# The end of a fused two-layer kernel: last block's mix moved ahead of its predecessor's second pair, its tiles turned by another path, the last pair's products reordered

## The chip, the core and the metric

The kernel runs on one core of one Trainium2 chip. The metric is device time in microseconds (us); the kernel before takes 696.96 us, the median of three runs (696.9 to 697.5).

## What is computed

Two layers follow one another on 8192 tokens of 512 features. The first adds a random-feature attention to its input and normalises; the second adds a magnitude (real and imaginary part of a product with cosines and sines) and normalises again.

```python
dot_products = jnp.einsum('...d,rd->...r', xw, ab[:, None] * gs)
correction = (0.5 * jnp.sum(xw * xw, axis=-1))[..., None] * (ab * ab)
return 1.0 / math.sqrt(NUM_RFS) * AB * jnp.exp(dot_products - correction)
...
return jnp.einsum('bsr,or->bso', feats, weights)
...
real = jnp.einsum('bti,io->bto', x, jnp.cos(theta + theta_noise))
imag = jnp.einsum('bti,io->bto', x, jnp.sin(phi + phi_noise))
return jnp.sqrt(real * real + imag * imag)
...
x = _layernorm(x + _L0_attn_ref(x, L0_attn_input_weights, L0_attn_xis, L0_attn_proj_matrix), axis=-1)
x = _layernorm(x + _L0_ffn_ref(x, L0_ffn_theta, L0_ffn_phi, L0_ffn_theta_noise, L0_ffn_phi_noise), axis=-1)
```

## The kernel before

The tokens are worked in 16 blocks of 512 (`NB` is 16), a block in four tiles of 128 tokens, the tiles in two pairs. In this document **e** is block 14, `NB - 2`, and **b** is block 15, the last. "(e,1)" is the second pair of e, "(b,0)" the first pair of b. Each engine has its own instruction list, written by hand, and runs it strictly in order; semaphores named after what they count join the lists. So a wait holds back all that stands behind it on its engine.

A block goes through these stages.

- **Mix** (L1001 to L1003, TensorE): features times weights, 12 matmuls for each tile into `token_ps`. VectorE adds the input (`residual1`, L1409) to give `z`, and takes its statistics (L1380, L1384) for the second normalisation.
- **Project** (L945 to L947, TensorE): the next block's features. The last block has none.
- **Turn**: the second layer needs `z` transposed. In all blocks from the third up to e, VectorE turns 32x32 squares of a pair (`turn_squares`, L1615), SyncE stores them to DRAM in four transfers (`store_squares`, L310) and fetches them back in three (`fetch_halves`, L317 to L319). In b, TensorE transposes each tile into `turn_ps` (`turn`, L1012, four transposes a tile) in between its other work.
- **Products** (L1119 to L1121, TensorE): a pair's two real and two imaginary tiles come from seven quarter products M1 to M7 instead of eight, six matmuls each (both operands are split into a high and a low part). Their left operands are quarters of the turned pair and four **half sums** of them (VectorE, L1620 to L1625). ScalarE rounds the high parts (L814 and L829; L819 and L825 in b), VectorE takes the low parts (L1276).
- **Joins** (VectorE): M1 is copied by ScalarE (L836, `copy_first`); then U, V, W and the four results C11, C12, C21, C22 are made by one addition each. `joined` counts them in order, so whoever waits for C21 waits for all that are joined before it. A bank of a product is free for the next pair when its joins have read it.
- **Magnitude and normalisation**: ScalarE squares a tile (L840), GpSimd or VectorE adds the squares (`pair_sum`, L470 on GpSimd), ScalarE takes the root (L718), the residual is added (L474 or L1605), VectorE takes statistics, GpSimd makes scale and shift for a pair in four small instructions (`pair_scale2`, L481 to L487), ScalarE scales into `o_tile` (`norm2`, L724) and SyncE stores.

In the last block the magnitude is worked tile by tile, and pieces of it go to all three engines (L879 to L929 on ScalarE, L527 to L548 on GpSimd, L1703 to L1846 on VectorE). TensorE's order at the end of before is: mix and project of e, pair (e,0), pair (e,1), mix of b with its turning in between, pair (b,0), pair (b,1).

## Time and profile before

| | us |
|---|---|
| median of three runs | 696.96 |
| lowest and highest run | 696.9, 697.5 |
| profiled execution, first to last instruction (span) | 694.6 |
| TensorE busy | 683.2 |
| VectorE busy | 598.5 |
| ScalarE busy | 461.6 |
| GpSimd busy | 202.2 |

The span is that of one profiled execution; it leaves out what lies before the first and behind the last instruction. A profile row gives a start in us from the span's start. A row that stands for several instructions covers them all. "Idle before" in brackets is how long the engine waited, and for whom.

### The profile page before, as it was taken

The page shows a single profiled execution, that of the slowest core. Times are in us where ns is not written, and L with a number is a line of the kernel's source. Part 1 is how long each engine was busy: PE and PEld are TensorE (multiplying, and loading weights), DVE is VectorE, ACT ScalarE, POOL GpSimd, SP SyncE. Part 2 cuts the span into 40 slices and gives each one's busy share as a digit, 9 for nine tenths or more (in the row PEclk, how much of TensorE's full clock was granted, in tenths as well). Part 3 has the DMA queues.
Part 4 walks back from the last instruction along what each step waited for, and adds up shares of the span by engine and source line. Part 5 has one row for each costly group of instructions (what it writes and reads, how often), then busy time and mean ns, then how long its engine had stood idle before and what let it go on. Part 6 is the DMA issues. An engine that isn't in the chain of part 4 may idle for free.

```text
span 694.6 us, 10316 instructions
## 1 busy us (share of the span) xinstructions
PE 683.2 (98%) x3026; PEld 564.2 (81%) x3026; DVE 598.5 (86%) x968; ACT 461.6 (66%) x698; POOL 202.2 (29%) x257
## 2 busy tenths in 40 slices
PE   9999999999999999999999999999999999999994
PEld 7888888878888888888888888888888888888883
DVE  6788999888889888889998887999888898988786
ACT  7868998395666758566674865757485675846446
POOL 5772304105041140503214040320405032050414
PEclk9999999999999999999999999999999999999998
DMA  8861031462826447182654708365380835534011
GB/s 311 234 137 61 15 121 63 116 202 43 211 82 146 157 113 204 31 214 88 142 160 104 213 23 216 94 123 179 95 222 15 213 104 121 181 79 119 0 61 61
DMA packets 168788, 88.10 MB, mean 127 GB/s; under 512 B 112576, under 2 KB 139200, under 8 KB 168768
## 3 DMA queue, kind: packets, MB, share of 16 engines
q1 hardware_dynamic: 167472, 85.51, 45.3%
q0 software_dynamic: 1152, 2.10, 1.8%
q10 hardware_dynamic: 144, 0.26, 0.1%
q8 instruction: 8, 0.13, 0.1%
q14 instruction: 12, 0.10, 0.0%
HBM read 57.41 MB, written 30.44 MB: 126 GB/s over the span
## 4 chain that ended last, share of the span: by engine, by line
PE 92%; DVE 3%; DMA 2%; issue 1%; ACT 1%; SPq 1%; POOL 0%; POOLq 0%; DVEq 0%; ACTq 0%
PE token_ps L1002 8%; PE token_ps L1003 8%; PE token_ps L1001 8%; PE token_ps L1119 6%; PE token_ps L1120 6%; PE token_ps L1121 6%; PE project_ps L945 5%; PE project_ps L947 4%; PE project_ps L946 4%; PE project_ps L1119 4%; PE project_ps L1120 4%; PE project_ps L1121 4%; PE turn_ps L946 3%; PE turn_ps L947 3%; PE turn_ps L945 3%; PE turn_ps L1120 3%
## 5 line engine op out<-in xcount | busy, mean ns | idle before, releaser
L470 POOL TENSOR_TENSOR plain_late<-plain_late 128x1024 f32<-128x1024 f32 x26 | 67.2, 2584 | 264.0 <-ACT plain_late L840 264.0
L1001 PE MATMUL token_ps<-W_hi,F_hi 128*128 128x512 f32 x256 | 99.7, 389 | 0.0
L1003 PE MATMUL token_ps<-W_hi,F_lo 128*128 128x512 f32 x256 | 99.6, 389 | 0.0
L1002 PE MATMUL token_ps<-W_lo,F_hi 128*128 128x512 f32 x256 | 99.6, 389 | 0.0
L724 ACT ACTIVATE o_tile<-plain_late,shift,rstd 128x512 f32<-128x512 f32 x56 | 42.6, 809 | 59.2 <-POOL shift L487 54.8
L718 ACT ACTIVATE plain_late<-plain_late 128x1024 f32<-128x1024 f32 x28 | 29.7, 1062 | 74.7 <-POOL plain_late L470 73.3
L1119 PE MATMUL token_ps<-T_hi,zT_hi 128*128 128x512 f32 x170 | 66.4, 390 | 0.5 <-DVE zT_lo L1276 0.5
L1121 PE MATMUL token_ps<-T_hi,zT_lo 128*128 128x512 f32 x170 | 66.2, 389 | 0.0
L1120 PE MATMUL token_ps<-T_lo,zT_hi 128*128 128x512 f32 x170 | 66.1, 389 | 0.0
L610 ACT ACTIVATE F_hi<-plain_expo,ab 128x512 fp32r<-128x512 f32 x62 | 44.7, 720 | 32.0 <-DVE plain_expo L1281 31.7
L840 ACT ACTIVATE plain_late<-plain_late 128x1024 f32<-128x1024 f32 x54 | 55.1, 1056 | 14.2 <-DVE plain_late L1693 11.1
L1276 DVE TENSOR_TENSOR zT_lo<-plain_zT_lo,zT_hi 128x1024 fp32r<-128x1024 f32 (+1 forms) x54 | 59.0, 1095 | 3.6 <-ACT zT_hi L814 0.5
L945 PE MATMUL project_ps<-xT_hi,gs_hi 128*128 128x512 f32 x144 | 56.8, 394 | 0.1
L1001 PEld LDWEIGHTS token_ps<-W_hi,F_hi 128*128 128x128 f32 x256 | 48.1, 188 | 10.0
L1003 PEld LDWEIGHTS token_ps<-W_hi,F_lo 128*128 128x128 f32 x256 | 48.1, 188 | 10.0
L947 PE MATMUL project_ps<-xT_hi,gs_lo 128*128 128x512 f32 x144 | 56.1, 390 | 0.0
L1002 PEld LDWEIGHTS token_ps<-W_lo,F_hi 128*128 128x128 f32 x256 | 48.1, 188 | 9.9
L946 PE MATMUL project_ps<-xT_lo,gs_hi 128*128 128x512 f32 x144 | 56.1, 389 | 0.0
L1409 DVE TENSOR_TENSOR z<-token_ps,x_tok 128x512 f32<-128x512 f32 x64 | 43.7, 685 | 13.2 <-PE token_ps L1003 11.5
L1436 DVE BATCH_NORM_STATS2 stats<-plain_late 128x6 f32<-128x512 f32 x56 | 37.4, 688 | 13.3 <-POOL plain_late L474 12.8
L1276 DVE TENSOR_TENSOR F_lo<-plain_F_lo,F_hi 128x1024 fp32r<-128x1024 f32 (+1 forms) x38 | 42.1, 1139 | 3.1 <-ACT plain_F_lo L611 3.1
L945 PE MATMUL turn_ps<-xT_hi,gs_hi 128*128 128x512 f32 x112 | 44.0, 393 | 0.0
(284 smaller groups left out, 1790.9 us busy)
## 6 DMA issues: line engine op xcount, KB each, us to landing
x_tok<-in_x SPq DMA_DIRECT2D x16, 1024.0 KB, 6.1
out_tokens<-o_tile SPq DMA_DIRECT2D x62, 256.0 KB, 2.8
plain_xT_lo<-in_xT SPq DMA_DIRECT2D x14, 1024.0 KB, 8.8
turned_pair<-plain_late SPq DMA_DIRECT2D x104, 128.0 KB, 2.8
plain_zT_lo<-turned_pair SPq DMA_DIRECT2D x26, 256.0 KB, 2.8
plain_zT_lo<-turned_pair SPq DMA_DIRECT2D x52, 128.0 KB, 2.8
norm_bc<-token_norms SPq DMA_DIRECT2D x15, 256.0 KB, 3.2
plain_T_hi<-in_gsT SPq DMA_DIRECT2D x4, 256.0 KB, 3.6
```

Source lines behind the costliest of these rows:

```text
L470: pool.tensor_tensor(parts[:, p, :, 0, :], parts[:, p, :, 0, :], parts[:, p, :, 1, :], ALU.add).then_inc(sum_made, 2)
L840: nc.scalar.activation(parts[:, p, i, :, :], parts[:, p, i, :, :], ACT.Square).then_inc(square_done, 2)
L945: nc.tensor.matmul(o, gs_hi[:, c, cols], rhs_hi[:, c, :], start=(c == 0), stop=False)
L946: nc.tensor.matmul(o, gs_hi[:, c, cols], rhs_lo[:, c, :], start=False, stop=False)
L947: return nc.tensor.matmul(o, gs_lo[:, c, cols], rhs_hi[:, c, :], start=False, stop=(c == C - 1))
L1001: nc.tensor.matmul(o, F_hi[:, c, cols], W_hi[:, c, :], start=(c == 0), stop=False)
L1002: nc.tensor.matmul(o, F_hi[:, c, cols], W_lo[:, c, :], start=False, stop=False)
L1003: return nc.tensor.matmul(o, F_lo[:, c, cols], W_hi[:, c, :], start=False, stop=(c == C - 1))
L1119: nc.tensor.matmul(o, left[0][i], right[0][i], start=(i == 0), stop=False)
L1120: nc.tensor.matmul(o, left[0][i], right[1][i], start=False, stop=False)
L1121: last = nc.tensor.matmul(o, left[1][i], right[0][i], start=False, stop=(i == H - 1))
L1276: return tt(dst, whole, hi.bitcast(F32), ALU.subtract)
```

## The change

It leaves all blocks before e as they are, and e too up to the joins of (e,0). From there on:

- TensorE takes the mix of b ahead of (e,1). The order is then mix and project of e, (e,0), mix of b, (e,1), (b,0), (b,1).
- b is turned as the other blocks are, by VectorE and DRAM; the 16 transposes of TensorE are gone. The turned squares go to the place of `xT`, the sum of b's first residual is written over its input (`last_z` is `x_tok[:, 1]`), and the turned second pair lands where the projection matrix was (`gs_hi`, `gs_lo`).
- The products of (b,1) come in the order M1, M6, M7, M4, M5, M2, M3, before M1, M2, M4, M6, M7, M5, M3; those of (b,0) in the order of all other blocks. Banks are those of all other blocks.
- `pair_sum(e, 1)` goes from GpSimd to VectorE. On ScalarE the root of tile 3 goes ahead of the last square.
- All lists from there to the end are written anew in `last_steps`.

```diff
-        QUARTER_ORDER_LAST = ["M1", "M2", "M4", "M6", "M7", "M5", "M3"]
+        QUARTER_ORDER_LAST = ["M1", "M6", "M7", "M4", "M5", "M2", "M3"]
-        JOIN_ORDER_LAST = ["U", "C11", "V", "C21", "C22", "W", "C12"]
+        JOIN_ORDER_LAST = ["U", "V", "C21", "C22", "W", "C11", "C12"]
...
+            store_squares(last, 0, last_squares)
+            fetch_halves(last, 0, last_raw)
+            store_squares(last, 1, last_squares)
+            store_out(last - 1, 0)
+            store_out(last - 1, 1)
+            fetch_halves(last, 1, last_raw)
+            store_out(last - 1, 2)
+            store_out(last - 1, 3)
...
-            pair_sum(b - 1, 1)
...
-            pool.wait_ge(square_done, 2 * C * NB + SQUARE_CREDIT - 1)
+            pool.wait_ge(square_done, 2 * C * NB + SQUARE_CREDIT - 2)
...
+                square_tile(e, 0, 1)
+                square_tile(e, 0, 0)
+                pair_roots(e, 0)
+                copy_first(e, 1)
+                norm2(e, 0)
+                norm2(e, 1)
+                round_halves(b, 0, last_hi, last_raw)
+                round_half_sums(b, 0, last_hi, last_raw)
+                square_tile(e, 1, 1)
+                copy_first(b, 0)
+                square_tile(e, 1, 0)
+                round_halves(b, 1, last_hi, last_raw)
+                round_half_sums(b, 1, last_hi, last_raw)
+                pair_roots(e, 1)
+                norm2(e, 2)
+                norm2(e, 3)
+                square_tile(b, 0, 1)
+                square_tile(b, 0, 0)
+                act.wait_ge(out_made, C * e + 3)
+                copy_first(b, 1)
...
-                square_part("C11", 0, 0)
+                square_part("C21", 1, 1)
...
-                square_part("C21", 1, 1)
                 square_part("C22", 1, 0)
+                square_part("C11", 0, 0)
+                root_tile(1, 1, last_sum_made, 1)
                 square_part("C12", 0, 1)
-                root_tile(1, 1, last_sum_made, 1)
                 root_tile(1, 0, sum_made, C * b + 3)
...
+                for name in QUARTER_ORDER_LAST:
+                    if name == "M1":
+                        pe.wait_ge(halves_lo_made, 2 * s + 2)
+                        pe.wait_ge(joined, joins_done(e, 1, JOIN_ORDER, "U"))
+                    else:
+                        if name == "M6":
+                            pe.wait_ge(half_sums_lo_made, 2 * s + 2)
+                        pe.wait_ge(joined, joins_done(b, 0, JOIN_ORDER, *BANK_READ[name]))
+                    one_product(1, name, last_hi, last_lo)
...
+                residual1(b, 1, 1, last_z)
+                turn_squares(b, 0, last_z, last_squares)
...
+                join_c12()
+                landed_half_sums(b, 1, last_raw)
+                split_halves(b, 1, last_hi, last_lo, last_raw)
+                pair_sum(e, 1)
+                join_u, join_v, join_w, join_c11, join_c12, join_c21, join_c22 = joins_of(b, 0)
+                join_u()
+                split_half_sums(b, 1, last_hi, last_lo, last_raw)
+                join_v()
+                pair_residual2(e, 1)
+                pair_stats2(e, 1, 0)
+                join_c22()
+                join_w()
+                pair_stats2(e, 1, 1)
+                pair_stats2_made(e, 1)
+                pair_moments2(1)
+                join_c11()
+                join_c21()
+                join_c12()
+                sum_tile(0, 1, 2)
+                sum_tile(0, 0, 4)
```

VectorE's list where b's first pair is joined, before. The first row is a low part of (b,1), L1620 to L1625 are its half sums, the others the joins of (b,0), in the order U, C11, V, C21, C22, W and C12:

```order
L1276 TENSOR_TENSOR zT_lo<-turn_ps1,zT_hi 128x256
L1667 TENSOR_TENSOR plain_late<-token_ps1,plain_late 128x512
L1682 TENSOR_TENSOR plain_late<-project_ps0,plain_late 128x512
L1620 TENSOR_TENSOR plain_zT_lo<-turn_ps1,plain_zT_lo 128x256
L1621 TENSOR_TENSOR plain_zT_lo<-turn_ps0,plain_zT_lo 128x256
L1623 TENSOR_TENSOR plain_zT_lo<-plain_zT_lo,turn_ps0 128x256
L1625 TENSOR_TENSOR plain_zT_lo<-turn_ps0,plain_zT_lo 128x256
L1674 TENSOR_TENSOR plain_late<-token_ps2,plain_late 128x512
L1693 TENSOR_TENSOR plain_late<-token_ps0,plain_late 128x512
L1698 TENSOR_TENSOR plain_late<-token_ps3,plain_late 128x512
L1678 TENSOR_TENSOR plain_late<-token_ps3,plain_late 128x512
L1687 TENSOR_TENSOR plain_late<-project_ps1,plain_late 128x512
```

There the joins of (b,0) share the list with work for (b,1) alone. The same place of the changed kernel (its own line numbers: L1620 is now every join, L1571 `pair_sum(e, 1)`, L1575 the residual of (e,1), L1406 and L1354 its statistics):

```order
L1246 TENSOR_TENSOR gs_lo<-plain_gs_lo,gs_hi 128x768
L1571 TENSOR_TENSOR plain_late<-plain_late 128x1024
L1620 TENSOR_TENSOR plain_late<-token_ps1,plain_late 128x512
L1246 TENSOR_TENSOR gs_lo<-plain_gs_lo,gs_hi 128x1024
L1620 TENSOR_TENSOR plain_late<-token_ps2,plain_late 128x512
L1575 TENSOR_TENSOR plain_late<-z,plain_late 128x1024
L1406 BN_STATS stats2<-plain_late 128x6
L1620 TENSOR_TENSOR plain_late<-token_ps3,plain_late 128x512 x2
L1406 BN_STATS stats2<-plain_late 128x6
L1354 BN_AGGR mv2<-stats2 128x2 x2
L1620 TENSOR_TENSOR plain_late<-project_ps0,plain_late 128x512
L1620 TENSOR_TENSOR plain_late<-project_ps1,plain_late 128x512
```

What moved: the sum of squares, the residual and the statistics of (e,1) now stand between the joins of (b,0), the last row of which is C21.

ScalarE's list from (b,1)'s half sums to the last scaling of a tile, before (L829 rounds, L840 squares a tile of (b,0), L836 copies M1, L879 are roots, L904 and L908 mean and variance of tile 1, L899 squares of one part, L918 scalings):

```order
L829 ACTIVATE zT_hi<-plain_zT_lo 128x1024
L840 ACTIVATE plain_late<-plain_late 128x2x512
L836 ACTIVATE plain_late<-project_ps0 128x512
L840 ACTIVATE plain_late<-plain_late 128x2x512
L879 ACTIVATE plain_late<-plain_late 128x512 x2
L904 ACTIVATE unused,mv2<-plain_late 128x512
L899 ACTIVATE plain_late<-plain_late 128x512
L908 ACTIVATE unused,mv2<-plain_late,mv2 128x512
L899 ACTIVATE plain_late<-plain_late 128x512 x3
L879 ACTIVATE plain_late<-plain_late 128x512 x2
L918 ACTIVATE o_tile<-plain_late,shift2,rstd2 128x512 x2
```

The same place of the changed kernel (L824 rounds, L729 is the root of (e,1), L735 scales tiles 2 and 3 of e, L833 squares (b,0), L829 copies M1, L898 roots, L911 and L915 mean and variance, L906 squares):

```order
L824 ACTIVATE gs_hi<-plain_gs_lo 128x1024
L729 ACTIVATE plain_late<-plain_late 128x1024
L735 ACTIVATE o_tile<-plain_late,shift2,rstd2 128x512 x2
L833 ACTIVATE plain_late<-plain_late 128x2x512 x2
L829 ACTIVATE plain_late<-turn_ps1 128x512
L898 ACTIVATE plain_late<-plain_late 128x512 x2
L911 ACTIVATE unused,mv2<-plain_late 128x512
L906 ACTIVATE plain_late<-plain_late 128x512
L915 ACTIVATE unused,mv2<-plain_late,mv2 128x512
L906 ACTIVATE plain_late<-plain_late 128x512 x2
L898 ACTIVATE plain_late<-plain_late 128x512
L906 ACTIVATE plain_late<-plain_late 128x512
```

What moved: e's last root and two scalings now stand ahead of the squares of (b,0) and of the copy of M1 of (b,1), and one root stands ahead of the last square.

## Rows read from the trace of the kernel before

**Rows 1.** The page: busy us, share of the span and instructions of each engine.

```profile
PE 683.2 (98%) x3026; PEld 564.2 (81%) x3026; DVE 598.5 (86%) x968; ACT 461.6 (66%) x698; POOL 202.2 (29%) x257
```

**Rows 2.** Timeline, TensorE, 633 to 685 us: start, duration, engine, line, operation.

```profile
633.26 0.39 PE L1119 MATMUL token_ps<-cos_hi,zT_hi 128*128 128x512 f32 x1
...
660.24 0.39 PE L1003 MATMUL token_ps<-W_hi,F_lo 128*128 128x512 f32 x1
...
668.57 1.03 PE L1012 MATMUL turn_ps<-ident,z 128*128 128x128 f32 x8
...
684.50 0.39 PE L1121 MATMUL project_ps<-low_sin_hi,zT_lo 128*128 128x512 f32 x1
```

**Rows 3.** Timeline, VectorE, block e: turning, residual, half sums, low parts.

```profile
617.94 1.25 DVE L1615 STREAM_TRANSPOSE plain_late<-z 128x1024 f32<-128x1024 f32 x1
619.11 1.18 DVE L1605 TENSOR_TENSOR plain_late<-z,plain_late 128x1024 f32<-128x1024 f32 x1
...
628.69 0.42 DVE L1620 TENSOR_TENSOR plain_zT_lo<-plain_zT_lo 128x256 f32<-128x256 f32 x1
...
630.34 0.96 DVE L1276 TENSOR_TENSOR zT_lo<-plain_zT_lo,zT_hi 128x768 fp32r<-128x768 f32 x1
...
631.88 1.22 DVE L1276 TENSOR_TENSOR zT_lo<-plain_zT_lo,zT_hi 128x1024 fp32r<-128x1024 f32 x1
...
634.84 0.43 DVE L1620 TENSOR_TENSOR plain_zT_lo<-plain_zT_lo 128x256 f32<-128x256 f32 x1 [0.56 <-DMA plain_zT_lo<-turned_pair]
```

**Rows 4.** Timeline, SyncE's queue, block e: stores and fetches of the turned pairs.

```profile
619.21 2.25 SPq L310 DMA_DIRECT2D turned_pair<-plain_late  x4
...
623.69 0.38 SPq L317 DMA_DIRECT2D plain_zT_lo<-turned_pair  x1
...
625.39 2.84 SPq L310 DMA_DIRECT2D turned_pair<-plain_late  x4
630.85 0.38 SPq L317 DMA_DIRECT2D plain_zT_lo<-turned_pair  x1
```

**Rows 5.** Timeline, ScalarE: rounding, two squared tiles, two scaled tiles.

```profile
628.31 0.83 ACT L814 ACTIVATE zT_hi<-plain_zT_lo 128x768 fp32r<-128x768 f32 x1
...
645.13 2.01 ACT L840 ACTIVATE plain_late<-plain_late 128x1024 f32<-128x1024 f32 x2 [0.19 <-DVE plain_late L1693]
...
658.25 1.52 ACT L724 ACTIVATE o_tile<-plain_late,shift,rstd 128x512 f32<-128x512 f32 x2 [0.21 <-POOL shift L487]
```

**Rows 6.** Timeline, GpSimd: first and last of a pair's four scale instructions; a tile's sum.

```profile
656.84 0.21 POOL L481 TENSOR_TENSOR var_eps<-mv,damp 128x2 f32<-128x2 f32 x1
...
658.02 0.20 POOL L487 TENSOR_TENSOR shift<-neg_mean,rstd 128x2 f32<-128x2 f32 x1
...
685.28 1.27 POOL L548 TENSOR_TENSOR plain_late<-plain_late 128x512 f32<-128x512 f32 x1 [0.52 <-ACT plain_late L899]
```

**Rows 7.** Timeline, VectorE, the end: joins of the last pair, and what follows.

```profile
680.91 0.69 DVE L1667 TENSOR_TENSOR plain_late<-token_ps,plain_late 128x512 f32<-128x512 f32 x1 [1.16 <-PE token_ps L1121]
681.52 0.68 DVE L1682 TENSOR_TENSOR plain_late<-token_ps,plain_late 128x512 f32<-128x512 f32 x1
682.26 0.69 DVE L1674 TENSOR_TENSOR plain_late<-token_ps,plain_late 128x512 f32<-128x512 f32 x1
...
685.24 0.69 DVE L1687 TENSOR_TENSOR plain_late<-project_ps,plain_late 128x512 f32<-128x512 f32 x1
685.85 0.68 DVE L1711 BATCH_NORM_STATS2 stats<-plain_late 128x6 f32<-128x512 f32 x1
686.63 0.69 DVE L1703 TENSOR_TENSOR plain_late<-plain_late 128x512 f32<-128x512 f32 x1
...
690.90 0.55 DVE L1388 TENSOR_SCALAR z<-plain_late,mv,rstd 128x512 f32<-128x512 f32 x1
```

**Rows 8.** Stretches of 1 us, TensorE: length, busy, granted clock, DMA share, GB/s.

```profile
687.00:688.00 1.00, 0.00 (x0) 0.92 0.00 0
688.00:689.00 1.00, 0.00 (x0) 0.50 0.00 0
```

634 lines of the change are left out of this document (271 added, 363 removed).

## The prediction

> **What bounds the kernel now.** Read the page's busy shares first: TensorE is busy 98% of the span [rows 1], and up to its last product it hardly ever waits. So only two things can shorten the kernel: less work or fewer gaps on TensorE, or a shorter tail behind its last product. Then the timeline of TensorE at the end [rows 2]: the pair (e,0) starts at 633.26, the transposes of b stand between its mix and its products, and the last matmul starts at 684.50 and ends at 684.89. Then VectorE's [rows 7]: the last join C12 starts at 685.24 and the last scaling ends at 691.45. The tail behind TensorE is thus 6.56 us of VectorE, ScalarE and GpSimd, and then the store. Then the other engines' rows for block e [rows 3 to 6], since they give the price of everything that the change puts into b. The span is 694.6 and the median 696.96, so 2.36 us lie around the span; I add the same after.
>
> **TensorE: 2.5 us less, if nothing else holds it.** Matmuls of 512 columns follow each other every 0.227 us (120 from 633.26 to 660.24). From 633.26 to 684.50 there are 216 of them and 16 transposes [rows 2]. Without transposes the rest of the list is 28 products of six matmuls (1.36 each) and four mixes of twelve (2.72 each), 48.97 us in all. From 633.26 that ends at 682.2, with the last matmul's own length at 682.4. Against 684.89 this is 2.5 us less: the slots of the transposes (the last eight take a row of 1.03 us, part of it under the next product [rows 2]) and the slower restart of matmuls behind each group. The mix of b now starts at 642.8, and its features are ready by then, since VectorE's list is unchanged up to the joins of (e,0). Moving it and the new banks cost nothing by themselves.
>
> **The turned pairs through DRAM: just in time.** The second tile of b is mixed at 648.4, its residual ends at 649.2, the turning of the pair takes 1.25 [rows 3] and ends at 650.5. In block e the store's first issue to the fetch's first issue took 4.5 (619.21 to 623.69) and, with more traffic beside it, 5.5 (625.39 to 630.85) [rows 4]; the fetch had landed 4.0 after its first issue (630.85 to 634.84, where VectorE waited for it) [rows 3, 4]. With 4.5 and 3.9 the pair (b,0) lands at 659.1; by the slower rows up to 661. TensorE wants its low parts at 663.2 and those of the half sums at 664.5. The half sums take 1.68, the low parts 0.88, and between them and the second low parts stand two joins: the first is ready at 661.8, the second at 664.1. This fits by 0.4 us, and a slow DMA costs TensorE 0.4 to 0.9, for which slack is to be had further on.
>
> A page of the Trainium skill speaks against this edit: "Vector Engine: DVE Perf Modes" names TensorE as the way for 128x128 transposes whose result may lie in PSUM ("Rules for kernel authors"). The rows agree that TensorE's way is short in latency, and by that rule alone the turning should have stayed there; no row shows what TensorE's own gap is worth once VectorE is full, which is what the following sum is about.
>
> **VectorE's queue: the bound that the change creates.** Before, the end of e and the work on b were spread over 50 us in which TensorE ran as well. Now b's turning, half sums and low parts, and all that (e,1) still needs of VectorE, `pair_sum(e, 1)` too, stand between joins. I went through the five lists from 641 on, row by row: an instruction starts when the one ahead on its engine lets it (a join every 0.61, the next one 0.77 behind its own operand [rows 7]) and 0.08 after what it waits for. The same walk over the kernel before ends the last scaling at 691.47, where the profile has 691.45. For the changed kernel it gives:
>
> - From the landing at 659.1 VectorE works without a stop: half sums 1.68, low part 0.88, joins C22 and W 1.22, low part 1.14, C11, a statistics pass (0.61 like a join [rows 7]) and C21 1.83, four small moments 0.48, C12 0.69. That is 667.05. The half sums of (b,1), landed long before, end at 668.6.
> - ScalarE squares (e,1) as its joins come and can round (b,1) only behind that (some 1.0 for a squared tile, 0.83 for the rounding [rows 5]): 669.3. VectorE loses 0.8 us there.
> - Then low part 0.88, `pair_sum(e, 1)` 1.10, U 0.61, low part 1.14, V 0.61, the residual of (e,1) 1.26 [rows 3], statistics, C22, W 1.83, statistics 0.77, moments 0.16, C11 0.61, C21 0.69: 9.66 us, so **C21 of (b,0) is joined at 679.1**.
> - TensorE has M1, M6 and M7 of (b,1) done at 676.8, and M4 needs the bank that C21 frees. It waits 2.3 us. Its last product ends at 684.85, where it ended before: **the 2.5 us are gone again.**
>
> **ScalarE and GpSimd: the tail gets longer.** The moments of (e,1) come at 677.84. GpSimd's four small instructions take 1.4 (656.84 to 658.22) [rows 6], so ScalarE scales tiles 2 and 3 of e from 679.3 to 680.8 (1.52 [rows 5]) and only then squares (b,0), until 682.7 (2.0 [rows 5]). VectorE, done with its joins at 679.7, waits for these squares, and the copy of M1 of (b,1) is behind them too: U of (b,1) starts at 683.4. Before it started at 680.91, and there it waited for its product; now M6 has been done since 675.6. The seven joins take 4.8, as before 5.0 (680.91 to 685.93), so C12 ends at 688.25 in place of 685.93: **2.3 us later.**
>
> Behind it the roots of (b,0) have also come later; the first ends at 683.8. GpSimd makes their residuals until 686.4, ScalarE the variance of tile 1 until 687.2, GpSimd its scale until 688.4, and only then the sum of squares of tile 3 (1.27 [rows 6]) until 689.65. ScalarE's list now has the root of tile 3 ahead of the last square, so that square starts at 690.3 and the sum of squares of tile 2 on VectorE at 690.99; before it was 686.63 [rows 7]. **Another 2.0 us later.** From there to the end of the last scaling it was 4.82 us (686.63 to 691.45 [rows 7]); the walk itself has 5.16, in both kernels. So the end comes at 695.8 to 696.15 in place of 691.45, 4.4 to 4.7 us later. I take 4.4, since it uses the measured tail.
>
> **The sum.** 694.6 + 4.4 + 2.36 = 701.4.
>
> **What is unknown.** The DMA path: a landing 0.5 earlier (the most that VectorE could use, since it waits 0.5 for it) takes 0.5 off, the slower store of [rows 4] adds 0.8, and with a fetch of 4.6 in place of 3.9, an estimate from the spread of the two stores, 1.5. The walk itself: 0.3 us off in its middle against the profile of before, so perhaps 1 us over this longer queue. TensorE's clock: before, it stayed at its upper level for some 2.9 us after the last matmul (0.92 in the stretch from 687, then 0.50, which is 1.2 GHz [rows 8]). A wait of 2.3 us is a little shorter, with one of over 2.9 the four products left would take 10.9 instead of 5.4 and C12 would end at 691; the tail hides all but 0.8 us of that, since the last square is late anyway. Instruction lists are longer by one unrolled block on TensorE; I count nothing for it.
>
> **The rivals.**
>
> - **As meant: the queues keep up.** Were C21 of (b,0) joined by 676.8, TensorE would end at 682.4, and with the tail of before, 6.56, the end would be at 689.0, 2.5 us sooner: 694.5. The point from which it decides is 2.3 us of VectorE's queue. For it: VectorE was idle at several places before (1.16 us ahead of 680.91 alone [rows 7]). Against it: the walk leaves only 1.3 us of idle time from 658.6 on, and none from 669.4 to 679.7. Chance 0.05.
> - **The wait on M4 comes, the tail stays as it was.** TensorE ends at 684.85, and ScalarE and GpSimd deliver as before: 697.0. It needs ScalarE to have squared (b,0) by 680, while its list puts e's scalings ahead. Chance 0.05.
> - **Forecast**, 4.4 us later, 0.72: 701.4, and by its own bounds 700.3 to 702.6.
> - **Slow turning**, the same with stores and fetches as in the slower rows: 5.9 us later, 702.9. Chance 0.11.
> - **The clock falls** during the wait for C21: 0.8 more, 702.2. Chance 0.07.
>
> **How the numbers follow.** The range, 699.7 to 703.4, holds the forecast and the last two rivals with 0.6 us to spare below and 0.5 above for the walk; the first two rivals lie outside. What counts as a change is 0.2%, or 1.4 us, about what a measurement of this kernel can tell from none. Faster 0.05, same 0.05, slower 0.90.
>
> **What would show it.** In the profile after: TensorE waits for VectorE's C21 at the first matmul of M4 of the last pair, 1.8 to 2.6 us; its last matmul starts at 684 to 685.5. VectorE has no idle time from 669.4 to 679.5, then waits some 2 us for the squares of (b,0). U of (b,1) starts near 683.4, the sum of squares of tile 2 near 691. ScalarE's two scalings of e end near 680.8. I am wrong if U of (b,1) starts before 681.5 or if the end of the last scaling is less than 6 us behind C12; and wrong in the first part if TensorE shows no wait behind M7 of the last pair.

## The result: 0.66% slower, and the profile after

The changed kernel takes 701.89 us (median of six runs, 700.98 to 703.06) against 697.68 for the kernel before measured beside it (six runs): the medians lie 4.2 us apart, and the ratio of the two, with a 95% interval, is 1.0066 (1.0053 to 1.0079). The profiled execution has a span of 699.0 (before 694.6).

The page's busy line answers [rows 1]: TensorE works 2 us less, VectorE 1.3 more, and the kernel is longer. Share of busy time does not explain this; the order of waits does.

```profile
PE 681.1 (97%) x3010; PEld 562.5 (80%) x3010; DVE 599.8 (86%) x969; ACT 459.8 (66%) x694; POOL 199.4 (29%) x256
```

Timeline of TensorE: its two waits from the mix of b on, and its last matmul ([rows 2] has that at 684.50).

```profile
643.21 0.47 PE L1007 MATMUL token_ps<-W_hi,F_hi 128*128 128x512 f32 x1 [0.34 <-DVE plain_late L1620]
...
679.36 0.50 PE L1119 MATMUL project_ps<-T_hi,gs_hi 128*128 128x512 f32 x1 [1.89 <-DVE plain_late L1620]
...
684.73 0.39 PE L1121 MATMUL turn_ps<-low_sin_hi,gs_lo 128*128 128x512 f32 x1
```

The wait of 1.89 is M4 of the last pair, for the join C21 of (b,0).

Timeline of VectorE: second residual of b, statistics of (e,0), the first half sum of (b,0), the first low part of (b,1), the last joins of (b,0), and the tail, which answers [rows 7].

```profile
648.95 0.69 DVE L1379 TENSOR_TENSOR x_tok<-token_ps,x_tok 128x512 f32<-128x512 f32 x1 [0.67 <-PE token_ps L1009]
...
654.73 1.29 DVE L1406 BATCH_NORM_STATS2 stats<-plain_late 128x6 f32<-128x512 f32 x2 [2.37 <-POOL plain_late L486]
...
659.71 0.41 DVE L1588 TENSOR_TENSOR plain_zT_lo<-plain_zT_lo 128x256 f32<-128x256 f32 x1
...
669.78 0.96 DVE L1246 TENSOR_TENSOR gs_lo<-plain_gs_lo,gs_hi 128x768 fp32r<-128x768 f32 x1 [1.02 <-ACT gs_hi L820]
...
678.05 1.25 DVE L1620 TENSOR_TENSOR plain_late<-project_ps,plain_late 128x512 f32<-128x512 f32 x2
...
682.16 0.69 DVE L1739 TENSOR_TENSOR plain_late<-plain_late 128x512 f32<-128x512 f32 x1 [2.26 <-ACT plain_late L833]
...
683.72 1.47 DVE L1620 TENSOR_TENSOR plain_late<-token_ps,plain_late 128x512 f32<-128x512 f32 x2
...
687.75 0.68 DVE L1620 TENSOR_TENSOR plain_late<-turn_ps,plain_late 128x512 f32<-128x512 f32 x1
...
691.04 0.69 DVE L1739 TENSOR_TENSOR plain_late<-plain_late 128x512 f32<-128x512 f32 x1 [2.01 <-ACT plain_late L906]
...
695.30 0.55 DVE L1358 TENSOR_SCALAR z<-plain_late,mv,rstd 128x512 f32<-128x512 f32 x1
```

Read them as one chain. VectorE has no gap between 669.78 and the end of C12 of (b,0) at 679.90; C11 and C21 are the two joins at 678.05. Behind them it waits 2.26 for ScalarE's squares, and ScalarE's own row says why they are late: it scales two tiles of e first, and had waited 6.63 us for GpSimd's shift.

```profile
679.66 1.52 ACT L735 ACTIVATE o_tile<-plain_late,shift,rstd 128x512 f32<-128x512 f32 x2 [6.63 <-POOL shift L499]
681.09 1.99 ACT L833 ACTIVATE plain_late<-plain_late 128x1024 f32<-128x1024 f32 x2
682.98 0.57 ACT L829 ACTIVATE plain_late<-turn_ps 128x512 f32<-128x512 f32 x1
```

So U of the last pair starts at 683.72 (before 680.91), its C12 at 687.75 (before 685.24), the last sum of squares at 691.04 (before 686.63) and VectorE's last scaling ends at 695.85 (before 691.45): 4.4 us. ScalarE's part of that scaling ends 0.12 us behind VectorE's in both kernels.

### The profile page after: what moved, and what is told of

The parts are those of the page before. It is cut to its first block and busy times, and to the rows that moved or that the text cites. A ratio compares the mean times of both kernels' runs of the same rounds, so it can differ in the third digit from the quotient of the medians.

```text
span 699.0 us, 10271 instructions
## 1 busy us (share of the span) xinstructions
PE 681.1 (97%) x3010; PEld 562.5 (80%) x3010; DVE 599.8 (86%) x969; ACT 459.8 (66%) x694; POOL 199.4 (29%) x256
## 5 line engine op out<-in xcount | busy, mean ns | idle before, releaser
L482 POOL TENSOR_TENSOR plain_late<-plain_late 128x1024 f32<-128x1024 f32 x25 | 65.8, 2633 | 261.9 <-ACT plain_late L833 261.9
L735 ACT ACTIVATE o_tile<-plain_late,shift,rstd 128x512 f32<-128x512 f32 x56 | 42.6, 809 | 70.4 <-POOL shift L499 60.3
L729 ACT ACTIVATE plain_late<-plain_late 128x1024 f32<-128x1024 f32 x28 | 29.7, 1062 | 74.4 <-POOL plain_late L482 71.7
L1620 DVE TENSOR_TENSOR plain_late<-token_ps,plain_late 128x512 f32<-128x512 f32 x112 | 74.0, 682 | 3.9
L833 ACT ACTIVATE plain_late<-plain_late 128x1024 f32<-128x1024 f32 x54 | 55.0, 1055 | 21.5 <-DVE plain_late L1620 21.2
L1119 PE MATMUL token_ps<-T_hi,zT_hi 128*128 128x512 f32 x162 | 63.1, 390 | 0.5 <-DVE zT_lo L1246 0.5
L1120 PE MATMUL token_ps<-T_lo,zT_hi 128*128 128x512 f32 x162 | 63.0, 389 | 0.0
L1121 PE MATMUL token_ps<-T_hi,zT_lo 128*128 128x512 f32 x162 | 63.0, 389 | 0.0
L1246 DVE TENSOR_TENSOR zT_lo<-plain_zT_lo,zT_hi 128x768 fp32r<-128x768 f32 (+1 forms) x54 | 58.8, 1089 | 3.4 <-ACT zT_hi L824 0.5
L1379 DVE TENSOR_TENSOR z<-token_ps,x_tok 128x512 f32<-128x512 f32 x60 | 40.9, 685 | 12.4 <-PE token_ps L1009 10.9
L1406 DVE BATCH_NORM_STATS2 stats<-plain_late 128x6 f32<-128x512 f32 x56 | 37.5, 688 | 14.9 <-POOL plain_late L486 14.4
```

What stands on the lines that cost most here:

```text
L482: pool.tensor_tensor(parts[:, p, :, 0, :], parts[:, p, :, 0, :], parts[:, p, :, 1, :], ALU.add).then_inc(sum_made, 2)
L1119: nc.tensor.matmul(o, left[0][i], right[0][i], start=(i == 0), stop=False)
L1120: nc.tensor.matmul(o, left[0][i], right[1][i], start=False, stop=False)
L1121: last = nc.tensor.matmul(o, left[1][i], right[0][i], start=False, stop=(i == H - 1))
L1246: return tt(dst, whole, hi.bitcast(F32), ALU.subtract)
L1620: tt(to, bank_of[name][:, :], to_it, ALU.add).then_inc(joined, 1)
```

## Experiments

Single profiled executions reach the second residual of b up to 3.7 us apart (648.95 in the changed kernel, 652.66 in pool_sum); the wait ahead of b's mix alone differs by up to 1.2 us between kernels whose lists are the same up to there. So I measure each by its **distance**: from the start of the second residual of b (648.95 above, where VectorE waits for TensorE's mix) to the end of the last scaling (695.30 + 0.55). In the changed kernel it is 46.90 us. The ratio beside it is the time against the kernel before. Here are the runs, with the change of the distance against the changed kernel that each theory's text stands for (mix_behind, a single run, is told at the end):

| run | ratio (interval) | distance | against changed | theory had |
|---|---|---|---|---|
| changed kernel | 1.0066 (1.0053 to 1.0079) | 46.90 | | |
| probe_queue | 1.0077 (1.0054 to 1.0099) | 48.10 | +1.20 | +1.2 |
| probe_idle | 1.0074 (1.0051 to 1.0098) | 46.96 | +0.06 | 0 |
| round_first | 1.0056 (1.0039 to 1.0073) | 46.15 | -0.75 | -0.75 |
| root_last | 1.0053 (1.0036 to 1.0071) | 45.62 | -1.28 | -1.4 |
| joins_first | 1.0092 (1.0071 to 1.0113) | 48.21 | +1.31 | +1.4 |
| three_orders | 1.0079 (1.0059 to 1.0098) | 46.04 | -0.86 | -2.1 |
| lists_anew | 1.0064 (1.0049 to 1.0078) | 46.33 | -0.57 | -5.6 |
| pool_sum | 1.0070 (1.0047 to 1.0094) | 47.42 | +0.52 | +0.5 |
| lists_apart | 0.9991 (0.9982 to 1.0000) | 41.35 | -5.55 | -5.5 |
| lists_apart_r | 0.9989 (0.9980 to 0.9998) | 41.60 | -5.30 | -5.9 |
| products_old | 1.0109 (1.0094 to 1.0125) | 48.53 | +1.63 | +0.3 |

The intervals are some 1 us wide on either side, so for the small edits it is the distance that decides, not the ratio: the times alone do not tell probe_queue from probe_idle, and for probe_idle and three_orders the ratio stands above the changed kernel's, with intervals that overlap. The distance comes from one profiled execution each. How well it repeats can be seen where lists are the same: from the second residual of b to M4 of the last pair the changed kernel takes 30.41 us, root_last 30.45 and probe_idle 30.45.

### Is VectorE's queue the bound, and where?

Two statistics passes whose result nobody uses, at two places. In probe_queue:

```diff
                 split_halves(b, 1, last_hi, last_lo, last_raw)
                 pair_sum(e, 1)
+                for k in range(2):
+                    nc.vector.bn_stats(probe_sink[:, k, :], last_z[:, 1, :])
```

> The changed kernel with 1.2 us of work more on VectorE whose result nobody uses: two statistics passes of 512 columns, between the sum of squares of (e,1) and the joins of (b,0), thus in the stretch in which the prediction found VectorE to be the bound. Theory: each microsecond there is a microsecond at the end. TensorE waits 3.1 us ahead of M4 in place of 1.9, the last scaling ends 1.2 us later, ratio 1.0083. Rival: the end is set by the chain of squares, sums and scales on ScalarE and GpSimd, and VectorE has slack; then as the changed kernel, 1.0066.

In probe_idle:

```diff
                 residual1(b, 1, 2, last_z)
+                for k in range(2):
+                    nc.vector.bn_stats(probe_sink[:, k, :], last_z[:, 1, :])
                 pair_stats2(e, 0, 0)
```

> The same 1.2 us of useless statistics passes on VectorE, but ahead of the statistics of (e,0) near 652.4, where it waited 2.4 us for GpSimd's residual. Theory: free, as the changed kernel, 1.0066 (no more than 0.2 us later), since VectorE is the bound only from the low parts of b on. Rival: VectorE is the bound in all of the last two blocks, and these cost as much as the others: 1.0083.

In distance, all of the 1.2 us comes out at the end in the first, none in the second. Timeline of TensorE in probe_queue, M4 of the last pair; the same row was a wait of 1.89:

```profile
683.00 0.50 PE L1120 MATMUL project_ps<-T_hi,gs_hi 128*128 128x512 f32 x1 [2.69 <-DVE plain_late L1621]
```

The wait is 2.69 and not the 3.1 expected, since M6 was held up too and M7 ends 0.4 us later; M4 itself starts 1.20 later, 31.61 behind the second residual of b in place of 30.41.

In probe_idle VectorE's own wait for GpSimd at the statistics of (e,0) shrank from 2.37 to 1.20 us and TensorE's for M4 stayed at 1.92. Of the two places, only the one behind the low part of (b,1) costs time.

probe_idle holds a second experiment that nobody planned. Right behind M4's wait the granted clock fell (0.74 in the stretch from 681, 0.50 in the next), and matmuls came 0.43 apart. Timeline of TensorE in probe_idle, and two stretches (length, busy, granted clock, DMA share, GB/s):

```profile
680.77 0.50 PE L1120 MATMUL project_ps<-T_hi,gs_hi 128*128 128x512 f32 x1 [1.92 <-DVE plain_late L1621]
...
682.04 0.63 PE L1121 MATMUL project_ps<-T_lo,gs_hi 128*128 128x512 f32 x1
...
687.74 0.39 PE L1122 MATMUL turn_ps<-low_sin_hi,gs_lo 128*128 128x512 f32 x1
```

```profile
681.00:682.00 1.00, 1.00 (x4) 0.74 0.00 0
682.00:683.00 1.00, 1.00 (x4) 0.50 0.22 84
```

From M4 to the last matmul it took 6.97 us and not 5.37, so TensorE ended 1.6 us later, and yet the end of the kernel moved by 0.06. So TensorE's end is not what sets the kernel's; what does is shown by the runs on the tail.

### ScalarE's part in that queue

```diff
                 square_tile(e, 1, 1)
                 copy_first(b, 0)
-                square_tile(e, 1, 0)
                 round_halves(b, 1, last_hi, last_raw)
+                square_tile(e, 1, 0)
```

> The changed kernel with ScalarE's rounding of the halves of (b,1) ahead of its square of the first tile of (e,1), as the halves have landed long before. VectorE idled 1.02 us for that rounding at 669.78. By the walk that idle time goes, the whole of VectorE's queue up to C21 of (b,0) moves by 0.75 us, TensorE's wait ahead of M4 shrinks from 1.9 to 1.1 us, and the end comes 0.75 us sooner: ratio 1.0055. Rival: the sum of squares of (e,1) needs that square and becomes what VectorE waits for instead; then nothing is gained, 1.0066.

Timelines of TensorE and VectorE in round_first:

```profile
680.06 0.50 PE L1119 MATMUL project_ps<-T_hi,gs_hi 128*128 128x512 f32 x1 [1.12 <-DVE plain_late L1620]
```

```profile
670.34 0.96 DVE L1246 TENSOR_TENSOR gs_lo<-plain_gs_lo,gs_hi 128x768 fp32r<-128x768 f32 x1
671.34 1.23 DVE L1571 TENSOR_TENSOR plain_late<-plain_late 128x1024 f32<-128x1024 f32 x1
```

The 1.02 of idle time ahead of the low part are gone. The sum starts 1.00 behind the low part in place of 0.87, so the rival holds for 0.13 us. M4 waits 1.12, and the end moves with it.

### The tail behind the last join

root_last puts the last square ahead of the root of tile 3, as before the change:

```diff
                 square_part("C11", 0, 0)
-                root_tile(1, 1, last_sum_made, 1)
                 square_part("C12", 0, 1)
+                root_tile(1, 1, last_sum_made, 1)
```

> The changed kernel with one part undone: on ScalarE the last square (C12 of the last pair) stands ahead of the root of tile 3 again. Theory (each engine's list is walked in order, and the tail is set by what stands ahead of what): the sum of squares of tile 2 on VectorE starts 2.0 us sooner in the walk and the end comes 1.4 us sooner, at about 694.5 instead of 695.85, so some 700.4 in time. Rival (the end is late only because TensorE waits 2 us for the bank of M4): that wait stays, so no change, 701.8.

The sum of squares of tile 2 starts 1.9 us sooner by distance and the end comes 1.28 sooner, although that sum now runs beside one of GpSimd and takes 1.25 in place of 0.69 (the next section has the reason). joins_first moves the joins of (b,0) ahead of what is left of (e,1):

```diff
                 join_v()
-                pair_residual2(e, 1)
-                pair_stats2(e, 1, 0)
                 join_c22()
                 join_w()
+                join_c11()
+                join_c21()
+                pair_residual2(e, 1)
+                pair_stats2(e, 1, 0)
                 pair_stats2(e, 1, 1)
                 pair_stats2_made(e, 1)
                 pair_moments2(1)
-                join_c11()
-                join_c21()
```

> The changed kernel with VectorE's joins C22, W, C11 and C21 of the first pair of the last block moved ahead of the residual and the statistics of block 14's second pair. It takes away TensorE's wait for M4 and leaves all else. Rival (that wait is the loss): TensorE ends 2.3 us sooner and so does the kernel, 699.5. Theory (ScalarE's list holds the squares of the last block behind block 14's two scalings, and these wait for the statistics moved back): TensorE's wait vanishes, its last product ends near 682.5, and yet the first join of the last pair starts 1.4 us LATER, near 685.1, and the kernel takes 1.4 us more, 703.3.

TensorE has no wait for M4 here, its last matmul starts at 683.20 (by distance 2.2 us sooner than in the changed kernel), and the end comes 1.3 us later than in the changed one. VectorE then waits 3.45 for the squares:

```profile
684.17 0.69 DVE L1739 TENSOR_TENSOR plain_late<-plain_late 128x512 f32<-128x512 f32 x1 [3.45 <-ACT plain_late L833]
```

This tells the two halves of the loss apart. The edit is no pure removal of the wait, since it pays for it with later statistics of (e,1). But TensorE ends 2.2 sooner and the kernel 1.3 later, because the squares, and the copy of M1 behind them, hang on those statistics by way of GpSimd and ScalarE. probe_idle is the counterpart: TensorE 1.6 later, the kernel the same.

### Two misses, and what they had in common

three_orders puts both edits together, and the squares of (b,0) ahead of the scaling of e:

```diff
                 pair_roots(e, 1)
-                norm2(e, 2)
-                norm2(e, 3)
                 square_tile(b, 0, 1)
                 square_tile(b, 0, 0)
+                norm2(e, 2)
+                norm2(e, 3)
```

> joins_first, and besides on ScalarE the squares of the last block's first pair ahead of block 14's last two scalings, and the last square ahead of the root of tile 3. Theory: together 2.1 us sooner than the changed kernel, of which 1.4 come from the last square and 0.7 from the two others together, though moving the joins alone costs 1.4 and moving the squares alone would bring only 0.1; the end of the last scaling near 693.8, the time near 699.8. Rival (the pieces simply add up): 1.4 sooner from the square, 1.4 later from the joins, 0.1 sooner from the squares, so the same as the changed kernel, 701.8.

It gained 0.86 and not 2.1. Timeline of GpSimd in three_orders, the last two of the four small instructions of a pair's scale, for (e,1):

```profile
680.43 1.25 POOL L496 TENSOR_TENSOR rstd<-var_eps,neg_half 128x2 f32<-128x2 f32 x1
681.81 0.65 POOL L499 TENSOR_TENSOR shift<-neg_mean,rstd 128x2 f32<-128x2 f32 x1
```

For (e,0) they took 0.70 and 0.20 in the same execution. (Durations on GpSimd are rough in such a profile, but the distance between the two starts grew by the same 0.55.) What ran beside them on VectorE were the sums of squares at 680.44 (0.68) and 681.71 (0.69). ScalarE waited 0.81 for the shift, and the scaling of e and the copy of M1 behind it came that much later. The last sum of squares, beside a sum of GpSimd, took 1.35 in place of 0.69; but root_last has 1.25 there and came out within 0.12 of its walk, so this explains little. Of the 1.2 us that are missing some 0.8 are thus accounted for, and the rest is open.

lists_anew takes new lists for the last two blocks on VectorE and ScalarE, and gives the sum of squares and the residual of (e,1) to GpSimd (L482 and L486 below):

```diff
             b = NB - 1
             pair_scale2(b - 1, 0)
+            pair_sum(b - 1, 1)
+            pair_residual2(b - 1, 1)
```

> The changed kernel with TensorE's list as it is, but the lists of VectorE, ScalarE and GpSimd from the mix of the last block on in another order: GpSimd makes sum of squares and residual of block 14's second pair, the turning of the second pair of the last block comes before statistics that can wait, the joins of the last block's first pair come before what the last pair does not need, and block 14's last two scalings come behind the squares. Theory: with the queues out of the way the 2.5 us that TensorE saves come through in part: the last product ends near 682.8, the last scaling near 690.3 against 691.45 in the kernel before, so 1.2 us sooner than before, 0.2%, ratio 0.998. Rival (the turning through DRAM costs what the transposes did, whatever the order): not sooner than the kernel before, ratio 1.000 or more.

Again a miss, by 5.0 us of distance. Timelines of GpSimd and of VectorE in lists_anew:

```profile
668.65 2.41 POOL L482 TENSOR_TENSOR plain_late<-plain_late 128x1024 f32<-128x1024 f32 x1 [7.03 <-ACT plain_late L835]
674.67 2.40 POOL L486 TENSOR_TENSOR plain_late<-z,plain_late 128x1024 f32<-128x1024 f32 x1 [3.60 <-ACT plain_late L731]
```

```profile
668.82 2.53 DVE L1590 TENSOR_TENSOR plain_gs_lo<-plain_gs_lo 128x256 f32<-128x256 f32 x1 [0.33 <-DMA plain_gs_lo<-turned_pair]
...
674.45 0.68 DVE L1622 TENSOR_TENSOR plain_late<-token_ps,plain_late 128x512 f32<-128x512 f32 x1
675.05 3.10 DVE L1248 TENSOR_TENSOR gs_lo<-plain_gs_lo,gs_hi 128x1024 fp32r<-128x1024 f32 x1
```

A half sum that takes 0.42 elsewhere takes 2.53 and ends 0.3 behind GpSimd's sum (671.06); a low part of 1.22 takes 3.10 and ends 1.1 behind GpSimd's residual (677.07). Both have two operands in SBUF. A join, which has one of them in PSUM, ran beside the start of that residual (674.45 to 675.13) at its usual 0.68. So in such a pair whoever started first went on, and the other stood. My walk knew nothing of it. With that rule in it (an instruction with two SBUF operands on VectorE and one of GpSimd exclude each other), the walk ends lists_anew at 695.3 instead of 689.8; measured, and counted from the changed kernel's second residual of b, it is 695.28. That is a fit after the fact, not yet a test.

The Trainium skill states this in "SBUF — State Buffer" ("SBUF: two separate sides"): VectorE and GpSimd share a pair of ports as an exclusive lock, taken by a VectorE instruction with two SBUF inputs when GpSimd's also reads SBUF, and the later one blocks until the first is done. The trace agrees, 2.53 for 0.42 and 3.10 for 1.22.

### The lock put to the test

pool_sum undoes one part of the change, the move of `pair_sum(e, 1)` off GpSimd. Without the lock that is a relief for VectorE; with it, a loss.

```diff
             b = NB - 1
             pair_scale2(b - 1, 0)
+            pair_sum(b - 1, 1)
...
                 split_halves(b, 1, last_hi, last_lo, last_raw)
-                pair_sum(e, 1)
```

> The changed kernel with one part undone: the sum of squares of (e,1) is GpSimd's again, as before the change; all else stays. GpSimd starts it at about 668.7 and holds it for 2.4 us, while VectorE comes to the low part of (b,1) at 669.4. Theory (VectorE's instructions with two operands in SBUF wait for a long one of GpSimd): that low part takes 2.5 us in place of 0.95, so VectorE gets back the 1.1 us of the sum only to lose 1.6, and the end comes 0.5 us later than in the changed kernel: ratio to the kernel before 1.007. Rival: the two engines do not hold each other up; then VectorE's full queue is 1.1 us shorter and so is the time, ratio 1.005.

Timelines of GpSimd and VectorE in pool_sum:

```profile
672.86 2.40 POOL L482 TENSOR_TENSOR plain_late<-plain_late 128x1024 f32<-128x1024 f32 x1 [10.77 <-ACT plain_late L834]
```

```profile
673.48 2.59 DVE L1247 TENSOR_TENSOR gs_lo<-plain_gs_lo,gs_hi 128x768 fp32r<-128x768 f32 x1 [1.03 <-ACT gs_hi L821]
```

The low part of 0.96 took 2.59, and the end came 0.52 later instead of 1.1 sooner. This is the one edit that tests the lock by itself. (Here too the granted clock fell behind M4's wait, of 2.39 us, and TensorE took 1.6 longer to its end, which again did not show.)

lists_apart is another set of lists, ordered by the walk with the lock in it, with nothing long on GpSimd beside b's halves. Its core on VectorE:

```diff
-                split_halves(b, 0, last_hi, last_lo, last_raw)
                 join_c22()
                 join_w()
-                split_half_sums(b, 0, last_hi, last_lo, last_raw)
                 join_c11()
-                stats1(b, 3, last_z)
                 join_c21()
...
+                split_halves(b, 0, last_hi, last_lo, last_raw)
                 join_c12()
-                landed_half_sums(b, 1, last_raw)
-                split_halves(b, 1, last_hi, last_lo, last_raw)
+                split_half_sums(b, 0, last_hi, last_lo, last_raw)
                 pair_sum(e, 1)
+                landed_half_sums(b, 1, last_raw)
+                pair_residual2(e, 1)
...
                 join_u()
-                split_half_sums(b, 1, last_hi, last_lo, last_raw)
-                join_v()
-                pair_residual2(e, 1)
                 pair_stats2(e, 1, 0)
-                join_c22()
-                join_w()
                 pair_stats2(e, 1, 1)
+                split_half_sums(b, 1, last_hi, last_lo, last_raw)
```

What it does is let (e,1) go first wherever TensorE does not yet wait, so that its statistics, and with them the scaling, are over 5 us sooner (673.41 against 678.14, less the 0.47 by which its second residual of b is later). ScalarE scales e and copies M1 of (b,1) ahead of the squares of (b,0), and takes the last root as root_last does.

> The three lists in a new order again, but now no long instruction of GpSimd (sum of squares, residual) runs while VectorE works on the halves of b: both, for the pair (e,1), are on VectorE. Where the sum of squares runs beside them as in the kernel called lists_anew (VectorE's 0.42 us half sum took 2.53 us beside GpSimd's sum at 668.65, its 1.22 us low part 3.10 us beside GpSimd's residual at 674.67), an instruction of VectorE with two operands in SBUF waited until GpSimd's was over. Theory: that waiting was what lists_anew lost. With it in the walk through the five lists, lists_anew ends its last scaling at 695.3 and not at 689.8, the changed kernel at 696.3, and this one at 690.5 to 691.0, where the kernel before has 691.45: 0.5 to 0.9 us sooner, a ratio to the kernel before of 0.999 (0.998 to 1.000), and some 5.5 us sooner than the changed kernel. Rival: what lists_anew lost lies in the lists or in the way through DRAM; then this one is late like it, at a ratio of 1.005 or more.

Timelines of VectorE and of TensorE in lists_apart:

```profile
666.51 1.23 DVE L1570 TENSOR_TENSOR plain_late<-plain_late 128x1024 f32<-128x1024 f32 x1
667.65 0.42 DVE L1587 TENSOR_TENSOR plain_gs_lo<-plain_gs_lo 128x256 f32<-128x256 f32 x1
...
684.52 0.69 DVE L1619 TENSOR_TENSOR plain_late<-turn_ps,plain_late 128x512 f32<-128x512 f32 x1 [0.74 <-PE turn_ps L1120]
...
690.22 0.55 DVE L1357 TENSOR_SCALAR z<-plain_late,mv,rstd 128x512 f32<-128x512 f32 x1
```

```profile
664.71 0.50 PE L1118 MATMUL token_ps<-cos_hi,zT_hi 128*128 128x512 f32 x1 [0.36 <-DVE zT_lo L1245]
...
684.02 0.39 PE L1120 MATMUL turn_ps<-low_sin_hi,gs_lo 128*128 128x512 f32 x1
```

The last join waits for TensorE again, and TensorE has no wait for M4. The last scaling ends at 690.77, within the 690.5 to 691.0 expected, though this execution reached b 0.47 later than the changed kernel's; the distance, which leaves that out, is 5.55 shorter than the changed kernel's, expected some 5.5. With 696.40 us it is 0.8% faster than the changed kernel and 0.1% faster than the one before, the latter at the edge of what its interval tells from nothing and less than the 0.2% that the prediction counts as a change. It differs from the changed kernel in many places, so it shows that the loss can be had back with b turned through DRAM; how much of the 5.5 us belongs to which move is not shown.

lists_apart_r also gives the residual of (e,1) to GpSimd, with the lists around it adjusted:

```diff
             pair_scale2(b - 1, 0)
+            pair_residual2(b - 1, 1)
...
-                pair_residual2(e, 1)
```

> As lists_apart, but the residual of (e,1) runs on GpSimd, at a moment when VectorE goes from low parts to joins (which read PSUM). By the walk it starts at 670.7, waits 0.7 us for VectorE's low part, and holds VectorE nowhere; the last scaling ends at 690.2 to 690.6, 0.4 us sooner than in lists_apart, ratio 0.998. Rival: VectorE arrives some tenths of a microsecond later than the walk has it, GpSimd's residual is first, and VectorE's next low part waits up to 2.4 us; then it is 1 to 2 us slower than lists_apart, ratio 1.001 to 1.003.

Neither came out in full. GpSimd's residual was the one that waited (2.98 us in place of 2.40, from 671.91), VectorE was held nowhere by it, but the gain of 0.4 did not come: distance 41.60 against 41.35, 696.23 us against 696.40. The two can't be told apart.

### Other parts of the change, undone

products_old restores the order that the last pair's products and joins had before:

```diff
-        QUARTER_ORDER_LAST = ["M1", "M6", "M7", "M4", "M5", "M2", "M3"]
+        QUARTER_ORDER_LAST = ["M1", "M2", "M4", "M6", "M7", "M5", "M3"]
-        JOIN_ORDER_LAST = ["U", "V", "C21", "C22", "W", "C11", "C12"]
+        JOIN_ORDER_LAST = ["U", "C11", "V", "C21", "C22", "W", "C12"]
```

> The changed kernel with one part undone: the products of the last pair in the order of before (M1, M2, M4, M6, M7, M5, M3), and its joins with them. M2 then needs the bank that C11 of (b,0) frees, right behind M1. By the walk TensorE waits for that from 674.2 to 678.5, 4.3 us, in place of 1.9 us ahead of M4, and its last product ends at 687.0 in place of 684.9. If the granted clock stays at its upper level over such a wait, the end comes only 0.3 us later than in the changed kernel, since the last pair's joins wait for ScalarE's copy anyway: 702.2, ratio 1.007. Rival: the clock falls in the wait, as it did some 3 us behind the last matmul of both kernels (0.92 in the stretch from 687 in the kernel before, then 0.50). Then the six products left take 16.3 us in place of 8.2, at worst, and the time is up to 707, ratio 1.010 to 1.015.

The wait is as expected, and the time of 703.97 (1.0109) lies at the low end of the rival's range, but its mechanism came only in part: the clock stayed up all through the wait and fell afterwards, for some of the products. Timeline of TensorE in products_old, and its stretches (length, busy, granted clock, DMA share, GB/s):

```profile
679.59 0.50 PE L1119 MATMUL project_ps<-cos_hi,gs_hi 128*128 128x512 f32 x1 [4.05 <-DVE plain_late L1620]
...
681.58 0.63 PE L1119 MATMUL project_ps<-T_hi,gs_hi 128*128 128x512 f32 x1
682.01 0.63 PE L1120 MATMUL project_ps<-T_lo,gs_hi 128*128 128x512 f32 x1
```

```profile
676.00:680.00 4.00, 0.41 (x2) 1.00 0.01 2
680.00:682.00 2.00, 2.00 (x7) 0.62 0.00 0
682.00:684.00 2.00, 2.00 (x6) 0.53 0.73 262
684.00:686.00 2.00, 2.00 (x10) 1.00 0.03 8
```

From 680.39 to 684.03 nine matmuls took 3.64 us instead of 2.04: 1.6 us lost, which with the 0.3 of the order itself would be 1.9, and 1.63 was measured. Here the loss shows, as TensorE is by then late enough that VectorE's U waits for it (1.05). The new order of products was worth its place: it makes a wait of 4.05 into one of 1.89.

mix_behind leaves the mix of b behind (e,1), with the turning through DRAM kept, and the lists of VectorE and ScalarE put into the order that this asks for; the diff shows TensorE's part:

```diff
                 first_pair(e)
-                pe.wait_ge(F_made, C * (b + 1))
-                for j in range(C):
-                    pe.wait_ge(joined, joins_done(e, 0, JOIN_ORDER, *BEFORE_MIX[j]))
-                    mix(b, j)
...
+                pe.wait_ge(F_made, C * (b + 1))
+                for j in range(C):
+                    pe.wait_ge(joined, joins_done(e, 1, JOIN_ORDER, *BEFORE_MIX[j]))
+                    mix(b, j)
```

> The changed kernel without its first part: b is turned by VectorE and DRAM, but its mix stands behind (e,1), as before. By the walk the pair (b,0) lands only at 671, TensorE waits some 11 us between mix and M1 of (b,0) (663.2 to 674.3), and the last scaling ends 4.5 us later than in the changed kernel, 706.3, if the clock comes back at once; with the clock at its lower level for the first products behind the wait 2 to 6 us more, up to 712. Rival: the changed kernel has lost so much in its queues that the place of the mix is worth little; then at most 1 us more than the changed kernel, 703 or less.

One run: 709.67 us, within the 708 to 712 that the theory gives with the lower clock, and far from the rival's 703. The span is 707.7, 8.7 longer than the changed kernel's. Timeline of TensorE in mix_behind, M1 of (b,0), and its stretches:

```profile
676.06 0.80 PE L1119 MATMUL token_ps<-cos_hi,zT_hi 128*128 128x512 f32 x1 [11.87 <-DVE zT_lo L1246]
```

```profile
664.00:668.00 4.00, 0.19 (x1) 1.00 0.48 128
668.00:676.00 8.00, 0.00 (x0) 0.50 0.97 234
676.00:680.00 4.00, 3.94 (x9) 0.50 0.20 75
```

So the way through DRAM needs the early mix: without it the kernel takes 8 us more than the changed one. The reverse, the early mix with TensorE's own transposes, was not run.

## Why the prediction was right, step by step

- **TensorE 2.5 us less, if nothing else holds it.** Right in kind, a little too much in size. From the last matmul of (e,0) to the last of all it was 41.94 us before (642.56 to 684.50); in joins_first, where no wait for M4 is left, it is 40.06 (643.14 to 683.20), 1.9 less. The wait at the mix takes most of the rest.
- **The mix of b costs nothing by itself.** Not quite: TensorE waits 0.34 there and restarts slower by 0.1, since VectorE comes to U of (e,0) at 642.38 and not at 640.94. "VectorE's list is unchanged" was true, but not enough: its data came later (the last section has what stands beside that).
- **Just in time through DRAM.** Store to fetch took 4.4 (650.95 to 655.32), expected 4.5. The landing was not waited for, since VectorE came to the half sums 0.6 later than in the walk (659.71).
- **VectorE's queue.** The walk put C12 at 667.05, the half sums' end at 668.6, the idle time for the rounding at 0.8, C21 at 679.1. Measured: 667.29, 668.76, 1.02, 679.30. probe_queue and probe_idle show that work in this queue comes out at the end in full behind the low part of (b,1), and not at all ahead of b's halves.
- **M4 waits 2.3, the gain is gone.** 1.89: the product ahead of it was 0.5 later than in the walk, C21 only 0.2. TensorE's end is 685.12 against 684.85. But that end does not set the kernel's: in probe_idle it came 1.6 later and cost 0.06. The prediction's own next step, the squares and the copy of M1, is the one that carries the time.
- **ScalarE and GpSimd lengthen the tail.** U of the last pair at 683.72 (683.4), the last sum at 691.04 (690.99), the end at 695.85 (695.8 to 696.15). joins_first moved the first of its two terms (U 1.33 later by distance, 1.4 in the walk) and root_last the second (the last sum 1.9 sooner, 2.0 in the walk). Both signs of being wrong stayed away: U did not start before 681.5, and from the end of C12 (688.43) to the end of the last scaling it was 7.4 us, not less than 6.
- **The sum.** The span came out as 694.6 + 4.4. The median is 0.5 us above 701.4, within the spread of runs; the kernel before, measured beside it, came out 0.7 above its 696.96 as well.
- **As meant.** The rival of a kernel 2.5 us faster needed VectorE to be 2.3 us sooner. lists_apart gives it more than that, and is faster than before by 0.8 us of distance from the end of (e,0) (642.69 to 690.77 against 642.56 to 691.45), not 2.5. TensorE's last matmul comes only 0.6 sooner (41.33 in place of 41.94): its waits at the mix and at M1 of (b,0) (0.60 and 0.36), a smaller one at M6 and the slower restarts behind each take the rest. The tail behind it is 0.2 shorter (6.36 in place of 6.56).
- **The rule on transposes.** By the Trainium skill's "VectorE: DVE Perf Modes" ("Rules for kernel authors") the turning should have stayed with TensorE. The runs do not show that it had to: lists_apart keeps it on VectorE and DRAM and is no slower than the kernel before (0.9991), so what the changed kernel lost lay in the lists and not in this way of turning. Nor do they show that DRAM is the better way, as no kernel has the early mix with TensorE's transposes.
- **The clock falls in the wait for C21.** It did not, at 1.89 us: the granted clock was 1.00 in the stretch from 678 to 680 and in the next. But the rival's condition, a wait of over 2.9, and its price do not stand. In probe_idle the clock fell behind a wait of 1.92, in probe_queue it stayed up with one of 2.69. Where it fell, it was back before the four products were done: TensorE lost 1.6 us and not 5.5, and the end 0.06 and not 0.8.

The walk lacked the lock between VectorE and GpSimd, and it was luck that this did no harm: the changed kernel has nothing long on GpSimd beside b's halves. The delay of block e, 0.45 us, was not in it either, and it fell mostly into the wait for M4, 0.4 shorter than forecast.

## What to carry to other kernels

When the bound engine is relieved by work given to engines that were idle on average, walk their lists instruction by instruction over the stretch in question, and start from the walk of the kernel as it is, until that one ends where its profile does. A wait that goes is worth nothing if the tail behind the last product hangs on another chain (joins_first, probe_idle); ask for both ends before moving anything. And before work goes from VectorE to GpSimd, or is put beside it, look for instructions of VectorE with two SBUF operands at that moment: here they cost 2.1 and 1.9 us each.

## What the runs showed of the hardware

**A lock between VectorE and GpSimd**, as above: 2.53 for 0.42, 3.10 for 1.22 and 2.59 for 0.96 us on VectorE; on GpSimd 1.25 for 0.70, 0.65 for 0.20 and 2.98 for 2.40. It works on small instructions too, and lengthened a chain of four by 1 us in three_orders.

**A slow store beside a transfer of the instruction queue.** In the changed kernel the first store of turned squares in block e takes 3.35 us to issue; the same store took 2.25 before [rows 4], and 2.25 in block b of the changed kernel too. Timeline of SyncE's queue:

```profile
619.13 3.35 SPq L314 DMA_DIRECT2D turned_pair<-plain_late  x4
...
650.95 2.25 SPq L314 DMA_DIRECT2D turned_pair<-plain_xT_lo  x4
```

The twelve other kernels of this study show 2.89 to 3.63 there. Within that store one transfer of the instruction queue falls, in the stretch from 620 to 621 of the changed kernel (packets, MB, share of 16 engines), which before has none there:

```profile
q8 instruction: 1, 0.02, 8.6%
```

The eleven stores of a first pair between 170 and 579 us took 2.24 to 2.29 in the changed kernel, with no such transfer in any of them. Behind the slow one the pair lands later, and VectorE begins its half sums of (e,1) at 636.28 instead of 634.84; U of (e,0) follows at 642.38 instead of 640.94, and TensorE's mix of b waits for that, 0.45 us with the restart. That the code fetch, and behind it the longer list, is the cause was not tested by itself. The prediction counted nothing for it.

**TensorE's clock** (1.00 is 2.4 GHz, 0.50 is 1.2 GHz). The length of a wait alone does not tell whether the clock falls, nor when. Each line is one profiled execution; "behind" counts from the end of the last matmul ahead of the wait.

| wait | where | what the granted clock did |
|---|---|---|
| 1.89 | changed kernel, M4 | stayed at 1.00 |
| 1.92 | probe_idle, M4 | fell 2.6 us behind, when matmuls ran again; TensorE 1.6 us longer, the end 0.06 |
| 1.93 | root_last, M4 | stayed at 1.00 |
| 2.39 | pool_sum, M4 | fell 3.4 us behind, when matmuls ran again; TensorE 1.6 us longer |
| 2.69 | probe_queue, M4 | stayed at 1.00 |
| 4.05 | products_old, M2 | fell 4.9 us behind, when matmuls ran again; 1.6 us lost |
| 11.87 | mix_behind, M1 of (b,0) | fell 3.9 us behind, in the wait; products at the lower level for another 5.6 us |

Behind the last matmul of all it fell 2.9 us later before [rows 8] and 3.1 in the changed kernel (0.59 in the stretch from 688). Whether it fell in the executions that were timed and not profiled is not on record.
